# Half projections behind both pairs, and the steps of a group norm two beats apart

## The reference

```python
xn = group_norm(x)                                  # layer norm in layer 2
q, k, v = split(xn @ w_qkv + b_qkv)                 # 8 heads of 16, or one of 128
o = softmax(q @ k.T * scale) @ v                    # 1024 x 1024 scores for each head
x = skip + o @ w_out + b_out                        # skip: x, or xn in layer 1
```

## Time and profile before

| | us |
|---|---|
| median of 3 runs | 2418.06 |
| lowest, highest | 2411.72, 2421.06 |
| the profiled execution, its own time | 2416.01 |
| its span in the trace | 2414.0 |
| PE busy | 2256.7 |
| DVE busy | 1794.8 |
| ACT busy | 1489.1 |

### The profile page before, as it was taken

The page is one execution under the profiler, slowest core; times in us unless marked ns, Lnnn a source line. Parts: engine busy times, 40 slices in busy tenths (PEclk is TensorE's granted clock), DMA queues, the critical chain, the costliest instruction groups (busy, mean ns, idle before and its releaser), DMA issues.

```text
span 2414.0 us, 34392 instructions
## 1 busy us (share of the span) xinstructions
PE 2256.7 (93%) x13298; PEld 1167.2 (48%) x13298; DVE 1794.8 (74%) x3350; ACT 1489.1 (62%) x1721; POOL 117.9 (5%) x118
## 2 busy tenths in 40 slices
PE   3999899999999899999999999999999999998999
PEld 2333333333543357433573336633376334744888
DVE  4898789888878877787767877788777875773443
ACT  1366566667567664677547774477745876467555
POOL 2000000000000000000000000000000000000000
PEclk7799999999999999999999999999999999999999
DMA  4211240303030304012030211303012030000000
GB/s 146 74 33 45 70 106 27 89 28 80 14 101 2 106 1 110 14 40 68 17 94 15 81 26 40 84 1 106 1 57 58 1 88 19 6 6 1 5 5 19
DMA packets 55218, 113.78 MB, mean 47 GB/s; under 512 B 6288, under 2 KB 9104, under 8 KB 54928
## 3 DMA queue, kind: packets, MB, share of 16 engines
q1 hardware_dynamic: 55056, 111.58, 17.4%
HBM read 55.98 MB, written 54.53 MB: 46 GB/s over the span
## 4 chain that ended last, share of the span: by engine, by line
PE 72%; DVE 19%; ACT 5%; issue 3%; DMA 0%; SPq 0%; POOL 0%; ACTq 0%; DVEq 0%; POOLq 0%
PE work L1205 17%; PE outs L1257 16%; DVE part_max L1001 13%; PE outs L1295 9%; PE pairs L1273 8%; PE pairs L1233 7%; PE pairs L1131 5%; PE pairs L1182 4%; ACT probs L879 2%; PE pairs L1176 2%; PE work L1182 1%; DVE stats L924 1%; PE pairs L1187 1%; DVE o_turn L1013 1%; ACT h L818 1%
## 5 line engine op out<-in xcount | busy, mean ns | idle before, releaser
L1001 DVE TENSOR_REDUCE part_max<-work 128x1 f32<-128x512 f32 x2048 | 1299.0, 681 | 324.0 <-PE work L1205 321.3
L879 ACT ACTIVATE probs<-pairs 128x1024 f32<-128x1024 f32 x1024 | 1016.9, 1022 | 431.2 <-PE pairs L1233 417.4
L1205 PE MATMUL work<-k_stack,q_stack 62*128 62x512 f32 x2048 | 785.0, 473 | 46.9 <-DVE part_max L1001 36.4
L1205 PEld LDWEIGHTS work<-k_stack,q_stack 62*128 62x128 f32 x2048 | 325.3, 189 | 681.5 <-DVE part_max L1001 552.1
L1233 PE MATMUL pairs<-q_stack,k_stack 64*128 64x512 f32 x2048 | 598.5, 443 | 10.7 <-ACT probs L879 8.0
L1257 PE MATMUL outs<-probs,v_heads 128*32 128x512 f32 x4096 | 555.6, 615 | 0.0
L886 ACT ACTIVATE probs<-pairs,neg_max 128x1024 f32<-128x1024 f32 x128 | 142.7, 1115 | 284.6 <-DVE neg_max L1033 284.6
L1233 PEld LDWEIGHTS pairs<-q_stack,k_stack 64*128 64x128 f32 x2048 | 262.1, 187 | 72.7 <-ACT probs L879 49.2
L1295 PE MATMUL outs<-v_full,probs 128*128 128x128 f32 x2048 | 252.8, 276 | 7.5 <-issue 7.5
L1295 PEld LDWEIGHTS outs<-v_full,probs 128*128 128x128 f32 x2048 | 246.5, 192 | 25.5 <-issue 17.1
L1033 DVE TENSOR_REDUCE neg_max<-pairs 128x1 f32<-128x1024 f32 x128 | 156.6, 1223 | 126.1 <-PE pairs L1273 125.9
(11 more groups left out here) (110 smaller groups left out, 959.5 us busy)
## 6 DMA issues: line engine op xcount, KB each, us to landing
k_scratch<-parts SPq DMA_DIRECT2D x96, 256.0 KB
q_scratch<-parts SPq DMA_DIRECT2D x96, 256.0 KB
k_stack<-k_scratch SPq DMA_DIRECT2D x64, 384.0 KB, 9.6
q_stack<-q_scratch SPq DMA_DIRECT2D x64, 384.0 KB, 10.9
q_stack<-shift_parts SPq DMA_DIRECT2D x256, 4.0 KB
tmp<-x SPq DMA_DIRECT2D x7, 512.0 KB, 4.0
out<-y SPq DMA_DIRECT2D x14, 256.0 KB, 2.1
w<-weights SPq DMA_DIRECT2D x1, 1152.0 KB, 7.0
```

What stands on the lines that cost most here:

```text
L879: nc.scalar.activation(probs[:, plan.prob[u], 2 * n:2 * n + 2, :], pairs[:, plan.half["pair", t], :, :], ACT.Exp, scale=HEAD_SCALE).then_i ...
L1001: nc.vector.tensor_reduce(part_max[:, r % 2, column:column + 1], bank_of(("tile", r, n)), AX_X, ALU.max, negate=True).then_inc(tile_max, 1)
L1205: nc.tensor.matmul(bank_of(("tile", r, n)), qs[rows, i, a, heads, P * t:P * (t + 1)], ks[rows, i, keys, heads, :], start=True, stop=True). ...
```

## The change

1. `NORM` gets an empty step between its steps, so that `stats`, `gn1`, `gn2` and `apply` stand two beats apart; `chain` and `project` skip empty names. `NORM_FAST` keeps one beat. It is used for layer 1 of images 0 and 7 and at the start. So layer 1 of images 1 to 6 has its steps at beats 7, 9, 11 and 13 in place of 7, 8, 9 and 10, and layer 3 of images 0 to 5 has `stats` to `apply` at 14, 16, 18 and 20 in place of 14 to 17, and its half projections at 21 to 26 in place of 18 to 23. Layer 0's list is as it was.
2. `narrow` also takes the half projections of head beats with fewer than four tiles: they use a bank of `work`.
3. `CHUNK_PATTERNS`: with 0 to 3 tiles both pairs and all tiles stand ahead of the chunk, with 4 the chunk stands behind the second tile.

The placement of tiles does not depend on any of this. With the new places of layer 3's projections, the head beats with half projections are, counted from the code: with three tiles 27 of k, 23 of q, 25 of v, 10 of out and one with out1 and q1; with two tiles one of q and one of v; with none 4 of k, 4 of q, 2 of v and one of out; with four or more 57.

```diff
--- before.py
+++ after.py
@@ -55,7 +55,8 @@
 PROJECTIONS = ("k0", "k1", "q0", "q1", "v0", "v1")
 SPLIT = ("k0", "k1", "q0", "q1")
 HALVES = PROJECTIONS + ("out0", "out1")
-NORM = ("stats", "gn1", "gn2", "apply")
+NORM = ("stats", "", "gn1", "", "gn2", "", "apply")
+NORM_FAST = ("stats", "gn1", "gn2", "apply")
 
 
 def half_of(name):
@@ -90,8 +91,8 @@
         self.place_chunks()
         self.tiles = self.place_tiles()
         self.shifted = set()
-        self.narrow = {c for b, (kind, _) in enumerate(self.beats) if kind == "full"
-                       for c in self.extra.get(b, []) if c[0] == "chunk" and c[1] in HALVES}
+        self.narrow = {c for b, (kind, _) in enumerate(self.beats)
+                       if kind == "full" or len(self.tiles.get(b, [])) < 4 for c in self.extra.get(b, []) if c[0] == "chunk" and c[1] in HALVES}
         self.order = self.first()
         for b in range(len(self.beats)):
             self.order += self.beat(b)
@@ -140,7 +141,7 @@
     def chain(self, beat, layer, image, names):
 
         for n in names:
-            for m in n.split("+"):
+            for m in n.split("+") if n else ():
                 self.put(beat, ("chunk", m, layer, image))
             beat += 1
         return beat
@@ -184,7 +185,7 @@
             self.chain(h(g0 + 1, 4), 0, i, ["out1"])
 
             late = i in (0, last)
-            self.chain(h(g0 + 1, 5 if i == 0 else 7), 1, i, NORM)
+            self.chain(h(g0 + 1, 5 if i == 0 else 7), 1, i, NORM_FAST if late else NORM)
             if late:
                 self.project(h(g1 - 1, 9 if i == 0 else 11), 1, i, one)
             elif g1 - 2 in FULLS_AFTER:
@@ -274,7 +275,7 @@
 
         order = [("load", 0), ("constants",), ("load", 1), ("merge",)]
         for i in range(2):
-            order += [("chunk", n, 0, i) for n in ("in", *NORM)]
+            order += [("chunk", n, 0, i) for n in ("in", *NORM_FAST)]
             if i == 0:
                 for n in PROJECTIONS:
                     order.append(("chunk", n, 0, i))
@@ -305,7 +306,7 @@
 
 
     PATTERNS = {0: "PCPV", 1: "TPCPV", 2: "TPCTPV", 3: "TPCTPTV", 4: "TPCTTPTV"}
-    CHUNK_PATTERNS = {0: "PCPV", 1: "TPCPV", 2: "TPCTPV", 3: "TPCTPTV", 4: "TPCTTPTV"}
+    CHUNK_PATTERNS = {0: "PPCV", 1: "TPPCV", 2: "TPTPCV", 3: "TPTPTCV", 4: "TPTCTPTV"}
 
     def beat(self, b):
         kind, n = self.beats[b]
```

## The result

| kernel | median, us | ratio to the kernel before | 95% interval |
|---|---|---|---|
| before (6 runs) | 2419.1 | | |
| changed (6 runs) | 2399.8 | 0.9919 | 0.9905 to 0.9933 |

The change makes the kernel 19.3 us faster, 0.8%. The forecast was 50.7 us. Its sign was right; its size was not.

A forecast was written before the change was run, and what follows sets the result against it. TensorE's queue was taken as the bound, VectorE as second limit. Terms 24.5 + 5.7 + 7.4 + 14.1 - 1.0 = 50.7 us gave a median of 2367 us from 2418.1, range 2338 to 2402.

The forecast's parts named there:

- Three-tile beats with a half: Beats of three or fewer tiles with a half projection: chunk behind all pairs in a work bank gains 24.5 us.
- The sum for one beat: Length of a three-tile beat with a half: 3.27 us for v, about 3.40 for q or k.
- Rival 1: Three banks with four users eat the order's gain; q, k and v halves stay at 3.57: 2383 us, chance 0.13.
- Rival 3: A chunk's bank comes back late, so three-tile beats with a half take about 4.4 us: 2442 us, chance 0.08.
- The four-tile order: 57 four-tile beats with a half: chunk behind the second tile gains 0.10 us each, 5.7 us.
- The norm steps: Norm steps two beats apart in layer 1, images 1 to 6, and layer 3, images 0 to 5: gain 7.4 us.
- k0 behind apply: Layer 3's k0 beat behind `apply`: k0 and k1 take 7.87 us against 11.16 in stage 8; 14.1 us in all.
- Rival 2: k0's wait behind `apply` only moves, as `apply` still stands one beat before it: 2378 us, chance 0.10.
- rival 4: One 3.42 us piece of low TensorE clock in each of 25 projection groups costs 43 us: 2410 us, chance 0.05.

The follow-up runs named there:

- e9: Changed kernel with the old `narrow` and, in beats of fewer than four tiles, the old order: 2391.2 us, ratio 0.9895.
- e1: Changed kernel, but the second head beat behind each full stretch keeps the old order and its half projection in `pairs`: 2384.6 us, ratio 0.9865.
- e6: Kernel before with one string changed, the chunk of a four-tile beat behind the second tile: 2407.8 us, ratio 0.9960.
- e2: Changed kernel with the old order strings and old `narrow`, so only the norm steps are spaced: 2401.4 us, ratio 0.9931.
- e8: e7 with the norm steps one beat apart again everywhere: 2393.0 us, ratio 0.9899.
- e7: Changed kernel, new treatment only for half projections, not second behind full stretches nor, under four tiles, behind turned outputs: 2372.8 us, ratio 0.9822.
- e5: Changed kernel, but in the second head beat behind a full stretch the chunk uses `pairs`, at its new place: 2392.2 us, ratio 0.9902.
- e4: Changed kernel, but in the second head beat behind a full stretch the chunk keeps its old place, with a work bank: 2385.5 us, ratio 0.9873.

## Why the forecast was wrong

Step by step, as the prediction put it:

- **Three-tile beats with a half, 24.5 us: failed.** Measured 6.6 (e9 against e1), and with the six beats behind full stretches -8.6 (e9 against the changed kernel; -6.7 by the ratios). The sum for one beat was good: q and k at 3.33 or 3.50 against 3.40, v1 of stage 8 at 3.36 against 3.27, v0 and k1 of stage 15, without tiles, at 2.95 and 2.71 against 2.73. (Its 1.05 for the chunk's own stretch is not in the earlier trace rows, whose row says 1.13; it is the time from start to start, as from 1131.65 to 1132.70 above.) What failed is the step that counts 46 q and k beats at 0.17 and 25 v beats at 0.30: one price for all beats of a kind. The price came from a beat in the middle of a stage whose DVE had little else to do. In beat 1 of stages 8, 10 and 12 and beat 25 of stages 6, 8, 10 and 12 the turned outputs stand ahead of the first maximum, and there the same edit loses 0.3 (k0, 3.57 to 3.88) and 0.8 (v0). v0 in beat 5 of stages 8, 10 and 12 loses 0.2, and k1 behind the six beats 0.36 in five stages (3.55 to 3.92, e9 against e1); their causes were not traced. In the six beats without pairs of their own it loses 2.7 us on average. The prediction took a half's beat by its tile count, and did not walk the list for beats in which the string means another order.
- **Rival 1** (the banks eat the gain of the order) is what the q, k and v halves of three tiles come to, 0.2 us in all where the forecast had 15.3, and its 2383 is near e1. It is luck in part that it fits: by rival 1 each of these beats stays at 3.57, but most win 0.05 to 0.3 and a few lose up to 0.8. For the changed kernel it is 17 us off, for it took the loss to be a gain missed, never a beat made longer.
- **Rival 3's mechanism** (a bank that comes back late) is what hit single beats, through the turned outputs and through waiting tiles, and in part through `rest`: with `rest` of q1 ahead of the turning v0 waits 0.96 us, without one k0 waits 0.40. (That is read from DVE's queue in two beats; no run takes `rest` alone away.) It did not lengthen every beat, as rival 3 had it.
- **The four-tile order, 5.7 us**: measured 9.2 (e6). An ordinary beat wins 0.05 where 0.10 was forecast; that this small gain is that of a partner for the pair's second half was not tested. The largest part, 4.4, came from `rest` behind one more maximum at a change of rounds, which the forecast had as "it allows that" and priced at nothing.
- **The norm steps and k0 behind apply, 7.4 + 14.1 = 21.5 us**: measured 15 to 18 alone (e2) and 20 beside the refined order (e8 against e7). The beats named came out right, k0 + k1 at 7.81 us against 7.87, the plain beat behind stats at 3.17 against 3.07. Rival 2 is out. The route was in part another one: k0 needed neither the new place nor the work bank for it (e2), and an estimated 9 to 12 of the 20 us are clock, which the forecast had counted only at k0. The new string takes 3.54 us for gn2 with four tiles, where the old one in e7 takes 3.06, which is the forecast's 2.70 + 0.35; that the small chunk now holds a bank later would explain it, but was not tested.
- **The clock, rival 4**: it did not cost what the rival had, for the mean granted clock is 0.978 in the changed kernel and 0.976 to 0.977 in the kernel before. But the pieces moved. In the changed kernel the piece at k0 behind apply in stages 8, 10 and 12 is gone, and pieces of 3.41 us (once 6.83) stand at the ends of five full stretches, as at 1258.70, and three more near the start of one. Those at the ends follow the row of waiting tiles, and e1, without that row, has none there; e5, where the chunk waits for no bank, still has some. By the page that gave the rival (the Trainium skill, TensorE: Matmul & The Clock Gate, A second HAM failure mode: psum-queue depth-cycling) short idles between groups, as PSUM banks are cycled, can make the clock oscillate. The short waits for a bank in ordinary beats did not do so here: stage 8 from beat 1 to beat 25, with waits of up to 0.96 us, has 1.00 (columns as in the earlier trace rows).

```profile
1056.00:1137.00 81.00, 75.04 (x441) 29.38 (x438) 65.11 (x123) 60.33 (x67) 5.95 (x7) 1.00 0.29 79
```

The measured terms add up: 15.3 to 17.7 for the spacing, 9.2, and 6.6 give 31 to 33 us for e1, which measured 32; less 15.2 for the six beats, that is 16 to 18 beside the 19 measured. The medians of the kernel before differ by about 2 us between the sets, so the account closes to its uncertainty. It is an account by kernels: each of these terms has its share of clock in it.

## What to carry to other kernels

When a queue's order is written by a rule, price the rule on the beats where it means something else (no pairs of its own, or another user of the same engine ahead) and not only on the common one; here six of 512 beats took back 13 to 15 of 32 to 34 us. A chunk that can run while tiles wait for banks is filler: keep it among the instructions that wait, not behind them (e4 shows that this holds here even when it uses a bank itself). And where a ring has one user more in a beat than it has banks, the last user waits for the whole chain of the first: price what can stand ahead of that chain in each beat, `rest` and the turned outputs here.

## Of the hardware

The granted clock makes a difference between kernels that the beats themselves don't have. Around 275 us the kernel before and e2 do the same work. The kernel before has 10.24 us at 0.50 there and e2 has over 20, first before, then e2:

```profile
276.85:287.09 10.24, 10.16 (x37) 3.99 (x38) 7.63 (x16) 4.09 (x4) 0.55 (x1) 0.50 0.01 2
```

```profile
275.00:295.30 20.30, 19.84 (x62) 7.62 (x54) 15.70 (x33) 5.81 (x7) 0.55 (x1) 0.50 0.00 1
```

e2's profiled span was 2406.2 beside a median of 2401.4. Of two kernels 5 us apart, one trace each doesn't tell which is faster. The lengths of single beats at the full clock are steadier: k0 in beat 1 of stages 8, 10 and 12 takes 3.87 or 3.88 us in both the changed kernel and e1.

The same shows between executions of one kernel. The kernel before took 2408.1 us at a mean granted clock of 0.982 and 2420.6 at 0.975, and e2 took 2397.0 at 0.983 and 2408.3 at 0.975. From these an estimate is 1.4 to 1.8 us for each 0.001. By it the clock makes up 9 to 12 of the 20 us between e7 and e8, 6 to 7 of the 15.2 between e1 and the changed kernel, and 7 to 9 of the 26 between e9 and the kernel before. So a kernel's order is worth its beats and what it does to the clock, and a forecast by beats alone leaves the second out.
